# Two edge sorts with runs of 16 records instead of 8, and block offsets added on GpSimd for 14 of 17 blocks of the first sort

## The reference

```python
x = x + _L0_gnn_ref(_layernorm(x), edge_index, edge_weight, Ws, bs, aw, ab)    # sums over edges by src
x = x + _L0_ffn_ref(_layernorm(x)[None], gate_w, gate_b, w1, w2, w3)[0]        # top 2 of 16 experts
x = x + _L1_gnn_ref(_layernorm(x), rel_emb, weight_neighbor, a, W3, ..., src, dst, etype)  # sums by dst
x = x + _L1_ffn_ref(_layernorm(x)[None], attention_mask, wr, br, w1, b1, w2, b2)[0]
```

## Time and profile before

| | us |
|---|---|
| median of 3 runs | 2223.59 |
| the runs | 2224.04, 2223.59, 2216.57 |
| the profiled execution | 2217.96 |
| its span | 2215.9 |

### The profile page before, as it was taken

The page is one execution under the profiler, slowest core; times in us unless marked ns, Lnnn a source line. Parts: engine busy times, 40 slices in busy tenths (PEclk is TensorE's granted clock), DMA queues, the critical chain, the costliest instruction groups (busy, mean ns, idle before and its releaser), DMA issues. The chain is left out here.

```text
span 2215.9 us, 33302 instructions
## 1 busy us (share of the span) xinstructions
PE 1600.6 (72%) x9301; PEld 1139.8 (51%) x9301; DVE 1663.4 (75%) x4230; ACT 1051.1 (47%) x2994; POOL 1259.5 (57%) x1217
## 2 busy tenths in 40 slices
PE   0477677776767766389999994477777777777198
PEld 0477344444544445289999993333333333334176
DVE  8998777777888767587878836688888888887601
ACT  0276254444444424212222224588888888874231
POOL 0288577777777750135666650277777777760042
PEclk9888776667575655599999996776777666768589
DMA  3012465455554452388999985277777777770432
GB/s 114 1 5 10 117 190 134 133 133 134 134 133 133 130 88 69 108 275 274 307 300 305 305 277 164 99 213 208 209 209 209 210 208 204 212 175 4 108 90 24
DMA packets 212758, 352.00 MB, mean 159 GB/s; under 512 B 45840, under 2 KB 123980, under 8 KB 212588
## 3 DMA queue, kind: packets, MB, share of 16 engines
q0 software_dynamic: 75616, 167.60, 30.2%
q1 hardware_dynamic: 136972, 182.41, 26.3%
HBM read 318.55 MB, written 31.34 MB: 158 GB/s over the span
## 5 line engine op out<-in xcount | busy, mean ns | idle before, releaser
L1173 POOL DMA_INDIRECT e_rows<-table,e_gidx x880 | 845.2, 960 | 268.1 <-issue 247.6
L1233 DVE TENSOR_TENSOR acc<-acc,e_psO 128x260 f32 (+1 forms) x880 | 461.6, 525 | 61.0 <-PE e_psO L1440 23.5
L1440 PE MATMUL e_psO<-e_rows,e_oh 128*128 128x260 f32 x880 | 384.1, 594 | 133.7 <-DVE acc L1233 133.4
L1440 PEld LDWEIGHTS e_psO<-e_rows,e_oh 128*128 128x128 f32 x880 | 229.8, 287 | 229.2 <-DVE acc L1233 107.5
L2273 PE MATMUL e_psO<-e_rows,e_oh 128*128 128x456 bf16 x440 | 210.9, 479 | 71.9 <-DVE acc L1233 69.9
L798 POOL DMA_INDIRECT records<-ordered,s_chunk x68 | 119.0, 1749 | 110.8 <-DVE s_chunk L625 80.9
L1410 ACT ACTIVATE e_rows<-e_psA 128x16 f32<-128x16 f32 x110 | 20.1, 183 | 309.5 <-DVE e_psA L1401 309.5
L2178 ACT ACTIVATE away<-iota_b,etype 128x200 bf16<-128x200 bf16 x440 | 165.2, 446 | 0.0
L2274 PE MATMUL e_psO<-e_rows,e_oh 128*128 128x256 bf16 x440 | 156.3, 355 | 0.0
L2275 PE MATMUL e_psO<-e_rows,e_oh 128*128 128x256 bf16 x440 | 156.2, 355 | 0.0
L1322 PEld LDWEIGHTS e_psA<-e_own_of_unit,e_ohT 128*128 128x128 bf16 x880 | 64.2, 105 | 174.9 <-ACT e_ohT L1275 96.7
(11 more groups left out here) (443 smaller groups left out, 3689.0 us busy)
## 6 DMA issues: line engine op xcount, KB each, us to landing
hot_run<-in_L_ffn_w_dram SPq DMA_DIRECT2D x107, 512.0 KB
XN<-in_L_ffn_w_dram SPq DMA_DIRECT2D x85, 512.0 KB
e_edge_row<-edge_rows SPq DMA_DIRECT2D x110, 256.0 KB, 4.0
e_edge_row<-edge_rows SPq DMA_DIRECT2D x110, 128.0 KB, 3.2
e_rows<-table,e_gidx POOLq DMA_INDIRECT x880
table<-frow SPq DMA_DIRECT2D x25, 192.5 KB, 2.3
table<-chunk_steps SPq DMA_DIRECT2D x25, 130.0 KB, 2.1
normed_rows<-Z SPq DMA_DIRECT2D x5, 642.5 KB
```

The source lines that it names most:

```text
L1173: pool.indirect_dma_start(out=rows[:, r, t, 0:width], out_offset=None, in_=table, in_offset=bass.IndirectOffsetOnAxis(ap=gidx[:, r, t:t + ...
L1233: v.tensor_tensor(d, d, psO[:, units * (r % (4 // units)) + j, 0:accw], ALU.add).then_inc(S["added"], 1)
L1440: return pe.matmul(out[:, 0:A0], oh[:, r, t, :], rows[:, r, t, :], start=start, stop=stop)
```

## The change

Three things change.

- `CK` goes from 8 to 16 with `COLS` still 32. So `KC` is 2, `ROWS` 122, `SROWS` 128, and a block goes out in two scatters of 128-byte runs instead of four of 64-byte runs, in both sorts. The arrays of `chunks` have half the elements. In sort 1 the two scatters of a block stand in one step.
- In sort 0, the first step of `select` (`run + base`, L645) is done by GpSimd for blocks 3 to 16, seven pairs. GpSimd waits for `reduced` (DVE has reduced the pair before, so `chosen` is free), adds, and signals `summed`, for which DVE waits in place of the sum. On GpSimd's queue the sum of pair k/2 stands ahead of the scatter of block k - 2.
- The buffer `blank` goes; the DRAM buffers are zeroed from `ordered`, and ACT waits for the end of that (`blanked`) before it writes `ordered`. The small arrays that shared `chunk_steps` get a buffer of sufficient size.

```diff
-    CK = 8
+    CK = 16
-    COLS = 4 * CK
+    COLS = 2 * CK
+    FIRST_PAIR = 3
...
+        def sum_places(self, eng, k, n, chosen):
+            blocks = slice(k, k + n)
+            return eng.tensor_tensor(chosen[:, 0:n, :, :], self.run[:, blocks, :, :],
+                                     self.base[:, blocks, :].unsqueeze(3).to_broadcast([EP, n, NB, CB]), ALU.add)
+
+        def pool_sums(self, pool, pair, chosen):
+            pool.wait_ge(self.reduced, pair + 1)
+            self.sum_places(nc.gpsimd, FIRST_PAIR + 2 * pair, 2, chosen).then_inc(self.summed, 1)
+
-        def select(self, link, k, n, chosen, hot=None):
+        def select(self, link, k, n, chosen, hot=None, dve=None):
...
-            link(v.tensor_tensor(picked, self.run[:, blocks, :, :], self.base[:, blocks, :].unsqueeze(3).to_broadcast(full),
-                                 ALU.add))
+            if dve is not None and k >= FIRST_PAIR:
+                dve.wait_ge(self.summed, (k - FIRST_PAIR) // 2 + 1)
+            else:
+                link(self.sum_places(v, k, n, chosen))
...
             link(v.tensor_reduce(self.pos[:, 0, at].rearrange("p (k c) -> p k c", c=CB),
                                  picked.rearrange("p k b c -> p k c b"), AX.X, ALU.max))
+            if dve is not None and n == 2:
+                dve.sem_inc(self.reduced, 1)
...
-        blank = sb("blank", [P, CHUNKS // P * CK * FIELDS[1]], c=c)
+        blank = ordered[:, :, :, :].rearrange("p k c f -> p (k c f)")
...
-                g.memset(blank[:, :], 0.0).then_inc(blank_set, 1)
                 g.memset(ordered[:, :, :, :], 0.0).then_inc(blank_set, 1)
                 pool.wait_ge(blanked, 48)
-                pool.wait_ge(es.addressed, 1)
                 for k in range(NBLK):
+                    if k % 2 == 0 and FIRST_PAIR + k + 1 < NBLK:
+                        es.pool_sums(pool, k // 2, chosen)
+                    if k == 2:
+                        pool.wait_ge(es.addressed, 1)
+                    if k >= 2:
+                        es.scatter(pool, k - 2, ordered)
+                for k in (NBLK - 2, NBLK - 1):
                     es.scatter(pool, k, ordered)
...
-                        es.select(link, 1, 2, chosen)
+                        es.select(link, 1, 2, chosen, dve=dve)
...
-                        es.select(link, k + 2, 2, chosen)
+                        es.select(link, k + 2, 2, chosen, dve=dve)
...
-                act.wait_ge(blank_set, 2)
+                act.wait_ge(blanked, 48)
...
-                            for late, some in enumerate(((0, 1), (2, 3))):
-                                if s - 1 - late in keep_at:
-                                    es1.scatter(pool, keep_at[s - 1 - late], ordered1, some)
+                            if s - 1 in keep_at:
+                                es1.scatter(pool, keep_at[s - 1], ordered1)
```

More of the change, by code:

```diff
@@ L637, in unit_starts @@
             v.tensor_scalar(self.unitf[:, 0:nu], self.unitf[:, 0:nu], -1.0, None, ALU.add).then_inc(self.unit_ready, 1)
-        def select(self, link, k, n, chosen, hot=None):
+        def sum_places(self, eng, k, n, chosen):
[6 more added lines that the diff above has]
+        def select(self, link, k, n, chosen, hot=None, dve=None):
             v = nc.vector
             at, blocks = slice(k * CB, (k + n) * CB), slice(k, k + n)
-            full = [EP, n, NB, CB]
             picked = chosen[:, 0:n, :, :]
-            link(v.tensor_tensor(picked, self.run[:, blocks, :, :], self.base[:, blocks, :].unsqueeze(3).to_broadcast(full),
-                                 ALU.add))
+            if dve is not None and k >= FIRST_PAIR:
+                dve.wait_ge(self.summed, (k - FIRST_PAIR) // 2 + 1)
+            else:
+                link(self.sum_places(v, k, n, chosen))
             if hot is None:
@@ L788, in keep_planes, with scatter @@
             v.tensor_copy(ordered[0:ROWS, k, :, 1], plane[:, :, 3]).then_inc(self.kept, 1)
-        def scatter(self, pool, k, ordered, some=range(4)):
+        def scatter(self, pool, k, ordered):
             n = COPIES[self.l]
[L793 to L797, removed]
+            pool.wait_ge(self.kept, k + 1)
+            if k >= n:
+                pool.wait_ge(self.scattered[k % n], 16 * KC * (k // n))
+            for j in range(KC):
                 pool.indirect_dma_start(
@@ L894, in build @@
         es.posf = elem
+        es.reduced, es.summed = sem("s0_reduced"), sem("s0_summed")
         es.picked, es.spaced, es.row_hot = sem("s0_picked"), sem("s0_spaced"), sem("s0_row_hot")
@@ L901, in build @@
         es.kept_numbers = sb("kept_numbers", [P, 4 * NBLK * NB], c=c)
-        es.steps = sb("chunk_steps", [P, NBLK * KC * NB], c=c)
+        spare = sb("chunk_steps", [P, max(NBLK * KC * NB, CH * A0 + H * O)], c=c)
+        es.steps = spare[:, 0:NBLK * KC * NB]
         rows = work[0:EP, 0:2 * CB * ROWS].rearrange("p (k c r) -> p k c r", k=2, c=CB)
@@ L911, in build @@
         rowb = sb("row_out0", [P, TILES // P, KINDS[0], P], BF16, c=c)
-        blank = sb("blank", [P, CHUNKS // P * CK * FIELDS[1]], c=c)
+        blank = ordered[:, :, :, :].rearrange("p k c f -> p (k c f)")
+        assert CHUNKS // P * CK * max(FIELDS) <= NBLK * COLS * FIELDS[0]
         assert 6 * NBLK * NB <= CB * ROWS
@@ L922, in build @@
         biasrow = sb("biasrow", [P, W0], c=c)
-        awprod = es.steps[:, CH * A0:CH * A0 + H * O].rearrange("p (h o) -> p h o", h=H)
-        assert CH * A0 + H * O <= NBLK * KC * NB
-        frow = es.steps[:, 0:CH * A0].rearrange("p (r a) -> p r a", r=CH)
+        awprod = spare[:, CH * A0:CH * A0 + H * O].rearrange("p (h o) -> p h o", h=H)
+        frow = spare[:, 0:CH * A0].rearrange("p (r a) -> p r a", r=CH)
         wloaded, wready, fready, fstored = sem("wloaded"), sem("wready"), sem("fready"), [sem(f"fst{r}") for r in range(CH)]
@@ L947, in _ @@
                 sp.dma_start(X[0:LAST, NT - 1, :], a["x"][(NT - 1) * P:N, :]).then_inc(xloaded, 16)
-                sp.wait_ge(blank_set, 2)
+                sp.wait_ge(blank_set, 1)
                 for l in range(2):
@@ L1805, in build @@
                 keep_at = {s + 3: k for s, k in mark_at.items()}
-                assert max(keep_at) + 2 < MT + 2 and KC == 4
+                assert max(keep_at) + 1 < MT + 2
                 pipeline, locate, back = ring(MT, WD)
```

## The result

The changed kernel takes 2229.52 us (median of 8 runs, 2226.16 to 2232.2) against 2222.34 for the kernel before on the same chip (8 runs, 2216.57 to 2224.88): 1.0042 times as long, interval 1.003 to 1.0054, or about 9 us; the medians differ by 7.2. Its profiled execution took 2230.1 us, with a span of 2228.0 against 2215.9.

A forecast was written before the change was run, and what follows sets the result against it. DVE was taken to bound the first sort and PE the expert stage; the terms summed to +8.3 us, making 2226.3 from the profiled 2217.96, or 2230 on the runs' mean, range 2209 to 2238.

The forecast's parts named there:

- sums leave DVE: First sort: seven offset sums of 125x1300 go from DVE, 1.54 us each with gap, -10.8 us.
- the port, seven adds: First sort: POOL's adds and DVE's two-input instructions exclude each other from SBUF, 2.6 us a sum, +18.2 us (chance 0.58).
- longer rows: First sort, DVE's row one-hot: padded rows grow from 109 to 122, +2.6 us up to mark 14 (block 14's product).
- chunk addresses: First sort, DVE's L621, L623 and L624: 1768 elements shrink to 884, 3 x 0.92, -2.8 us.
- Free passage: First sort's marks: POOL's adds run beside DVE at no cost, total -9.9 us, 2211.5; chance 0.28.
- Half passage: First sort: adds give way at element or burst level, about 1.3 us each, total -0.8 us, 2220.6; chance 0.14.
- Where the price falls: First sort: some of L685, L694 and L698 last 2 to 3 us more; only the small conversions run beside an add.
- The sort's end: After mark 14 (block 14's product): PE's blocks of 122 columns make +0.7 us; DVE's read-back wait goes, -0.5 us.
- Scatters that do nothing, adds late: First sort: scatters at 3.5 us make POOL's adds late, DVE loses about 1 us a pair, 2218.5; no separate chance.
- Expert stage: Second sort, 922 to 1337 us: block 0's longer one-hot +0.3 us, PE's placements with 122 columns of weights +0.6 us.

The follow-up runs named there:

- e3: Changed kernel with two buffers for `chosen`, the masking product signalling `reduced`, so adds run beside DVE's reductions; phase 1 ends at 243.0 us, whole 2389.62 against 2403.72 before.
- e6: Changed kernel with runs of 8 again (`CK = 8`), adds still on POOL; phase 1 ends at 272.3 us, whole 2407.86 against 2391.31 before.
- e4: Changed kernel with all sums on DVE, while POOL does the seven adds into an idle buffer nobody reads; phase 1 ends at 272.5 us, whole 2415.03.
- e5: Changed kernel with all sums on DVE and two unread POOL memsets in place of each add; phase 1 ends at 260.4 us, whole 2398.2.
- e0: The kernel before, run again unchanged for a trace from another chip; phase 1 ends at 256.3 us, whole 2393.84 against 2391.31 in its job.
- e7: The arrangement of e3 (adds beside the reductions) with runs of 8; phase 1 ends at 257.2 us, whole 2391.68 against 2391.31 before.
- e1: Changed kernel with runs of 16 kept but all sums back on DVE; phase 1 ends at 257.8 us, whole 2404.33 against 2403.72 before.
- e2: Changed kernel with each of the seven POOL adds done twice, DVE waiting for the second; phase 1 ends at 279.6 us, whole 2424.42 against 2403.72 before.
- e8: Changed kernel with the reduction itself signalling `reduced`, without a separate increment on DVE; phase 1 ends at 263.8 us, whole 2400.63 against 2388.9 before.

## Why the prediction held

I forecast 8.3 us more and about 2230 us; the profiled spans differ by 12.1 and the medians by 7.2. For the profiled execution I had 2226.3 and it took 2230.1; 3.3 us of its surplus are those of phase 6, in code that the change doesn't touch. Phase 1 and the expert stage, where my terms lie, make +7.9. By its own steps, in phase 1 up to mark 14 (it comes 8.3 us later though the selects start 0.2 earlier, so +8.5 is to be accounted for):

| step | predicted | measured |
|---|---|---|
| sums leave DVE | -10.8 | -10.8 |
| the port, seven adds | +18.2 | +18.15 |
| longer rows | +2.6 | +2.6 (1289 to 1424 ns x12, 2991 to 3327 x3) |
| chunk addresses | -2.8 | -2.8 (2.00 to 1.08 us, three times) |
| signal instruction | not foreseen | +1.2 (0.15 us idle before L673, eight times) |
| sum | +7.2 | +8.4 |

*The port's cost* held as a total, by a different sum, and that the mean is 2.59 us where I took 2.6 is in part luck. An add takes 2.36 us (e3), below my 2.7 scaled from the earlier trace rows; the prices run from 2.19 to 3.20. The 2.77 on average in the kernel after is no hold-up: the five adds that directly follow a scatter are recorded at 2.94, from 0.55 us before the scatter's record ends, and those of e6 at 2.90 though DVE stands still beside them. What I had read from the earlier trace rows in one direction holds in the other as well: DVE stands still until the add is done. Which of the two began first does not settle it, since in e4 instructions of DVE that began up to 0.7 us before the add's record stood still too. Free passage (0.28) would have left L713 at 1826 ns; it is at 2148, and e4 shows the price with nobody reading the result. Half passage (0.14) is excluded too: the smallest of the seven prices is 2.19 us, where it had 1.3.

The Trainium skill, page "SBUF — State Buffer", section "Who interferes with whom", has a VectorE instruction with two SBUF inputs and a reading GpSimd instruction exclude each other. By that rule, the trace agrees for the five adds that meet such an instruction, 13.76 of the 18.15 us; the other two stop a conversion with one input, 4.39 us.

*Where the price falls* I had only partly right. I wrote that the small conversions run beside an add. Two of the seven adds stop a conversion of 0.19 us for 2.2 us (L675 and L673 at 2.38); e5 stops them even with memsets.

*The sort's end.* Predicted +0.7 for PE's longer rows and -0.5 for the read-back: +0.2 together. Measured from mark 14 to the barrier: 64.8 before, 64.65 after, -0.2. The read-back's wait is gone as said, and DVE's wait at the last mark grew from 2.7 to 3.1 us. Up to the last mark it is +0.7 (10.7 to 11.4 us), but e0, with the shorter rows, took 11.5, so this term can't be told from what two traces of one kernel differ by.

*Two small slips in the working.* 195 elements more of L728 are 0.20 us by its own row, not 0.18, and a quarter of 0.58 is 0.145, not 0.16. Neither moves the forecast.

*Scatters that do nothing, adds late.* The 34 scatters take 1.82 us each (rival: 3.5), and DVE never waits for an add. e6 shows that this rival was real for runs of 8.

*Expert stage.* Predicted +0.9, measured -0.2. Its two terms exist: the placements go from 28.0 to 28.5 us over 425 instructions, and PE's wait in block 0 from 3.32 to 3.7 us. That is +0.8 to +0.9 in these two rows, and some other part of the stage, which I have not found, is 1.1 us shorter.

The largest thing that I missed does not show in the total. I treated seven adds at 2.6 us as the price of the idea; e3 shows that it was the price of their place. The same adds, one step earlier, cost nothing that the trace shows. I had the row for it: in the earlier trace rows the scatter under the reduction is the shortest of the three.

## What to carry to other kernels

Before moving an operation from a busy VectorE to an idle GpSimd, ask which VectorE instructions it will run beside: here a 1.5 us sum moved to GpSimd cost VectorE 2.6 us on average beside instructions with two SBUF inputs and small conversions, and nothing under a reduction with one input. Place it by its signal (and give it a buffer of its own, so that it may start there), and make GpSimd's queue short enough that it comes at that moment; each without the other gave no gain (257.2 us in e7 and 264.3 in the kernel after, against 256.2 before). Time lost on one engine before a dense stretch of TensorE can come back in part through TensorE's clock, so read the loss at the phase's end as well as at the instruction. It need not: from mark 14 to the end of phase 1 e1 takes 66.0 us, e4 and e5 60.5, but e2 65.0 and e6 65.8.

## What the runs showed of the hardware

- A GpSimd memset does not lengthen VectorE's two-input instructions (984, 1423 and 1825 ns in e5, as alone), nor do they hold it up. The row of POOL L650 in e5's timeline holds two memsets. The second has 1.18 us, as alone, and lies wholly beside the product L715:

```profile
108.25 1.55 POOL L814 DMA_INDIRECT records<-ordered,s_chunk  x1 [0.30 <-issue]
109.23 3.00 POOL L650 MEMSET late<- 125x1300 f32 x2
110.71 1.82 DVE L715 TENSOR_TENSOR work<-cols,field 125x1600 f32<-125x1600 f32 x1
```

- The record of an add or memset on GpSimd that directly follows a scatter begins 0.5 to 0.6 us before the scatter's ends, and is longer by about as much: in the rows above the scatter ends at 109.80, and the first memset, from 109.23, has 1.76 us. The adds have 2.94 for 2.36 (kernel after, e4) and 2.90 in e6. This is not time that VectorE took from them.
- Small integer conversions on VectorE, with one input, are stopped by a GpSimd add (0.19 to 2.38 us) and by memsets (0.19 to 0.94 on average in e5), while a reduction, with one input too, is not (2.59 against 2.54 us). What sets the conversions apart no run shows.
- A semaphore increment as an instruction of its own on VectorE left 0.15 us of idle time before the next one, each time (1.2 us for eight in the kernel after; gone in e8).
- PE's 50 instructions of 122 columns after mark 14 took 8.41 us in e1, where the granted clock was 0.63 over just these, a mixture of 1.2 and 2.4 GHz, and 5.44 in e4, where it was 1.00, all at 2.4 GHz. PE had waited 5.14 us before them in e1 and 2.77 in e4.
